# Second feed-forward matmul: the loads of every odd chunk moved from the SyncE and ScalarE queues to the GpSimd queue

## Chip, cores and metric

The kernel runs on all 8 cores of one Trainium2 chip, one batch element per core, with no traffic between the cores. The metric is the device time of the slowest core in microseconds (us). One execution in a comparison is one such time.

## What is computed

One adaLN layer on x of shape 8 x 2048 x 1024 (batch, tokens, width). The part that matters here is the end of it, the feed-forward block with quantized operands:

```python
def bitlinear(x, W, b):
    w_scale = clip(mean(abs(W)), EPS)
    Wq = clip(round(W / w_scale), -1, 1) * w_scale          # ternary weights
    x_scale = clip(max(abs(x), axis=-1), EPS)
    xq = clip(round(x * (127 / x_scale)), -128, 127) * (x_scale / 127)
    return einsum('bnd,hd->bnh', xq, Wq) + b

h = layernorm(x) * (1 + cb) + sb
h = gelu(bitlinear(h, W1, b1))          # 1024 -> 4096
x = x + gb * bitlinear(h, W2, b2)       # 4096 -> 1024, the part around the change
```

Before it stand the modulation vectors (silu(c) @ wmod), a first layernorm and a gated recurrence over the tokens (three 1024 x 1024 projections and a scan).

## The kernel before

Each core works on its element transposed: the width lies on the 128 partitions, the 2048 tokens in the free dimension. `Prog` collects the instructions of each engine as a list written out by hand; `p.on(engine, fn, wait, inc)` appends waits on semaphores and then the instruction. An engine works strictly through its list, so an instruction whose wait isn't met holds up all behind it on that engine. `dma=True` only takes away the serializing wait that ScalarE, VectorE and GpSimd put around their own compute instructions. A DMA adds 16 to its semaphore when it has landed.

The second matmul multiplies the quantized hidden activations (4096 x 2048, bf16, 16 MB, kept in HBM as `h1qsp`) with the ternary weights (4096 x 1024, kept as `w2qsp`). The eight PSUM banks `PB` hold two output blocks of 128 rows (`d0`, `d1`) times four token tiles of 512. So the output is made in four groups `gi` = 0 to 3 of two blocks each, and each group reads all 32 chunks `kc` of the contraction again.

- Group 0 (matmuls at L1292) is made while VectorE quantizes the activations pair by pair; each pair is stored to `h1qsp` (L1279).
- Groups 1 to 3 (matmuls at L1332) only load and multiply. A chunk is 8 matmuls of 128 x 128 by 128 x 512 and needs two loads: its activations `H1Q2[pp]` <- `h1qsp[kc]`, 128 x 2048 bf16, 512 KB, issued by SyncE at L1319 (in the profile: X<-h1qsp, engine SPq), and its weights `W2R[pp]` <- `w2qsp[kc]`, 128 x 1024 bf16, 256 KB, issued by ScalarE at L1321 (M<-w2qsp and RB<-w2qsp, engine ACTq). There are four buffers of each, `pp` = `kc % 4`. The load of chunk kc waits for the matmuls of chunk kc-4; the first four of a group wait for the last matmul of the group before, and in group 1 also for the last stores of `h1qsp`.
- After each group follows an epilogue of eight tiles `ei` over two output buffers `OUTP`: VectorE scales PSUM, ScalarE applies gate and bias, VectorE adds the residual, GpSimd issues the store to `out_img` (L1368). Tile ei waits for the store of tile ei-2, which used the same buffer. The first matmul of the next group waits until VectorE has read the last bank.

So at the end of a group SyncE prefetches four activation chunks at once, while ScalarE comes to the four weight loads only behind its eight epilogue activations, and GpSimd has nothing but the stores.

Of the kernel before, what the change touches and what calls it, by code (L numbers as in the profile page):

```python
# [106 lines left out]
def build_nc():  # L107
    nc = bass.Bass("TRN2", target_bir_lowering=False)
    p = Prog()
# [39 lines left out]
    h1qsp = nc.dram_tensor("h1qsp", [HC, 128, L], BF16, kind="Internal").ap()  # L149
# [80 lines left out]
    for _j, _v in enumerate(_cvals):  # L230
# [8 lines left out]
    PB = [nc.alloc_psum_tensor(f"PB{i}", [128, NT], F32).ap() for i in range(8)]  # L239

    semnames = ["sBR", "sMD", "sM1", "sM2", "sM3", "sLXa", "sLXb", "sCN", "sWMa", "sWMb", "sLWa", "sLWb",
                "sMW", "sW1a", "sW1b", "sW2", "sW2b", "sW2c", "sW2d", "sLWc", "sLWd", "sSP", "sSPa", "sSPb", "sRDa", "sRDb",
                "sFINa", "sFINb", "sMM", "sDV", "sAC", "sPL",
                "sVq", "sSq", "sPq", "sTAP", "sH1a", "sH1b", "sW1c", "sW1d"]
    sems = {s: nc.alloc_semaphore(s) for s in semnames}
# [1 line left out]
    for s in semnames:  # L247
# [7 lines left out]
         inc=("sCN", 16), dma=True)  # L255
    p.on("scalar", lambda E: E.dma_start(out=CPB[:], in_=cpack_b),
         inc=("sCN", 16), dma=True)
    p.on("scalar", lambda E: E.dma_start(out=IDNF[:], in_=idnf),
         inc=("sCN", 16), dma=True)
# [3 lines left out]
    for k in range(KC):  # L263
# [3 lines left out]
             wait=w, inc=(sx, 16))  # L267
        p.on("vector", lambda E, k=k: E.tensor_copy(chunk(X, k), xstg[k % 2]),
             wait=[(sx, p.cnt[sx])], inc=("sDV", 1))
# [3 lines left out]
         wait=[("sCN", cn_all)], inc=("sAC", 1))  # L273
# [143 lines left out]
    for t in range(48):  # L417
# [4 lines left out]
            inc=("sMD", 1) if t == 47 else None)  # L422
    mm_modc = p.cnt["sMD"]
    p.on("vector", lambda E: E.tensor_copy(MODC[:], PB[2][:, 0:48]),
         wait=[("sMD", mm_modc)], inc=("sDV", 1))
# [43 lines left out]
    def ws2_fin(E):  # L469
# [10 lines left out]
         wait=[("sDV", ws2_done)])  # L480
    p.on("tensor", lambda E: E.matmul(PB[7][:, 1:2], ONESRf[:],
                                      WSrow[0:1, 3:4], start=True, stop=True),
         inc=("sMM", 1))
# [11 lines left out]
    for k in range(KC):  # L495
        wv = [("sDV", modc_done)] if k == 0 else []
        for j in range(NNT):
# [3 lines left out]
                wait=wv if j == 0 else [],  # L501
                inc=("sM3", 1) if (k == KC - 1 and j == NNT - 1) else None)
# [17 lines left out]
    for k in range(KC):  # L520
        wv = [("sM3", st1_mm[k - 2])] if k >= 2 else []
        p.on("vector", lambda E, k=k: E.tensor_tensor(
            sq1[k % 2], chunk(X, k), chunk(X, k), ALU.mult),
            wait=wv, inc=("sDV", 1))
        sqdv = p.cnt["sDV"]
        for j in range(NNT):
# [4 lines left out]
                wait=[("sDV", sqdv)] if j == 0 else [],  # L531
                inc=("sM3", 1) if j == NNT - 1 else None)
# [28 lines left out]
    for j in range(NNT):  # L561
# [3 lines left out]
            wait=[("sAC", rstd1_ac)] if j == 0 else [],  # L565
            inc=("sM3", 1) if j == NNT - 1 else None)
# [10 lines left out]
    for j in range(NNT):  # L577
# [3 lines left out]
            wait=[("sAC", bc1e_ac)] if j == 0 else [],  # L581
            inc=("sM3", 1) if j == NNT - 1 else None)
# [12 lines left out]
    for k in range(KC):  # L595
        wv = [("sDV", bc1_done)] if k == 0 else [("sAC", p.cnt["sAC"])]

        def ln_apply_v(E, k=k, src=X):
# [6 lines left out]
            wait=[("sDV", p.cnt["sDV"])], inc=("sAC", 1))  # L605
# [79 lines left out]
    if DEBUG_TAPS:  # L685
        p.on("gpsimd", lambda E: E.dma_start(out=tap_hln, in_=Hh[:]),
             wait=[("sAC", p.cnt["sAC"])], inc=("sTAP", 16), dma=True)
        p.on("gpsimd", lambda E, v=p.cnt["sTAP"]: E.wait_ge(sems["sTAP"], v))
        p.on("gpsimd", lambda E: E.dma_start(out=tap_mod, in_=MODC[:]),
             inc=("sTAP", 16), dma=True)  # L690
# [160 lines left out]
    for k in range(KC):  # L851
        wv = [("sDV", bc2_done)] if k == 0 else []

        def h2_v(E, k=k):
# [6 lines left out]
            wait=[("sDV", p.cnt["sDV"])], inc=("sAC", 1))  # L861
        acn = p.cnt["sAC"]
        M1n = XS(4096, 6144)
        if k == 0:
# [3 lines left out]
                wait=[("sAC", acn)], inc=("sDV", 1))  # L868
        else:
# [3 lines left out]
                wait=[("sAC", acn)], inc=("sDV", 1))  # L873
# [4 lines left out]
        inc=("sDV", 1))  # L878
# [100 lines left out]
    if DEBUG_TAPS:  # L979
        p.on("gpsimd", lambda E: E.dma_start(out=tap_xq, in_=Hh[:]),  # L980
             wait=[("sDV", p.cnt["sDV"])], inc=("sTAP", 16), dma=True)
        def tapstm(E):
# [4 lines left out]
             inc=("sTAP", 16), dma=True)  # L987
        p.on("gpsimd", lambda E, v=p.cnt["sTAP"]: E.wait_ge(sems["sTAP"], v))
        p.on("gpsimd", lambda E: E.dma_start(out=tap_bs[:, L:2 * L], in_=BS1[:]),
             inc=("sTAP", 16), dma=True)  # L990
# [46 lines left out]
    for hc in range(HC):  # L1037
        if hc + 2 < HC:
            emit_tern(hc + 2)
        for j in range(NNT):  # L1040
            jp = (hc * NNT + j) % 4
            gidx = hc * NNT + j
            for k in range(KC):
                wv = []
                if k == 0:
                    wv = [tern_dvs[hc]]
                    if gidx == 0:
                        wv += [("sDV", xq_done)]
                    if gidx >= 4:
# [6 lines left out]
                     wait=wv, inc=("sMM", 1) if k == KC - 1 else None)  # L1056
# [5 lines left out]
                wait=[("sMM", mmn)], inc=("sDV", 1))  # L1062
# [6 lines left out]
                wait=[("sDV", dvn)], inc=("sAC", 1))  # L1069
        gelu_acs.append(p.cnt["sAC"])  # L1070
        H1T = H1Tp[hc % 2]
        if hc == 0:
# [3 lines left out]
                 wait=[("sAC", gelu_acs[-1])], inc=("sDV", 1))  # L1076
# [22 lines left out]
        inc=("sDV", 1))  # L1099
# [95 lines left out]
    for gi, (d0, d1) in enumerate([(0, 1), (2, 3), (4, 5), (6, 7)]):  # L1195
# [111 lines left out]
        else:  # L1307
            for kc in range(HC):
                pp = kc % 4
                srd = ["sRDa", "sRDb", "sW1a", "sW1b"][pp]  # L1310
                wv = []
                if kc < 4:
                    wv = [("sMM", last_mm)]
                    if gi == 1:
                        wv += [("sH1a", p.cnt["sH1a"]),
                               ("sH1b", p.cnt["sH1b"])]
                elif (gi, kc - 4) in mm_vals:
                    wv = [("sMM", mm_vals[(gi, kc - 4)])]
                p.on("sync", lambda E, kc=kc, pp=pp: E.dma_start(  # L1319
                    out=H1Q2[pp], in_=h1qsp[kc]), wait=wv, inc=(srd, 16))  # L1320
                p.on("scalar", lambda E, kc=kc, pp=pp: E.dma_start(  # L1321
                    out=W2R[pp], in_=w2qsp[kc]), wait=wv, inc=(srd, 16),
                    dma=True)
                rdn = p.cnt[srd]
                mmw = [(srd, rdn)]
                if kc == 0:
                    mmw += [("sDV", bank_free_dv)]
                for nt in range(NNT):
                    for di, d in enumerate((d0, d1)):
                        p.on("tensor",  # L1330
                             lambda E, kc=kc, pp=pp, nt=nt, di=di, d=d:
                             E.matmul(PB[4 * di + nt][:, :],  # L1332
                                      W2R[pp][:, d * 128:(d + 1) * 128],
                                      H1Q2[pp][:, nt * 512:(nt + 1) * 512],
                                      start=(kc == 0), stop=(kc == HC - 1)),
                             wait=mmw if (nt == 0 and di == 0) else [],
                             inc=("sMM", 1) if (nt == NNT - 1 and di == 1)
                             else None)
                mm_vals[(gi, kc)] = p.cnt["sMM"]
# [145 lines left out]
```

How the kernel before makes its waits and increments, by code:

```python
    def on(self, eng, fn, wait=(), inc=None, dma=False):  # L40
        sems = self.sems
        serialized = (eng in ("vector", "scalar", "gpsimd")) and not dma
        for (s, v) in wait:
            if v > 0:
                self.ops[eng].append(lambda E, s=s, v=v: E.wait_ge(sems[s], v))
        if inc is not None:
            sname, amt = inc
            val = self.inc(sname, amt)
            if fn is None:
                self.ops[eng].append(
                    lambda E, s=sname, a=amt: E.sem_inc(sems[s], a))
            elif serialized:
                def run(E, f=fn, s=sname, a=amt):
                    f(E)
                    E.ser_flush_wait()
                    E.sem_inc(sems[s], a)
                self.ops[eng].append(run)
            else:
                self.ops[eng].append(
                    lambda E, f=fn, s=sname, a=amt: f(E).then_inc(sems[s], a))
            return val
        assert fn is not None
        self.ops[eng].append(fn)
        return None
# [1 line left out]
    def barrier(self):  # L66
        for e in ENGINES:
            self.inc("sBR", 1)
        target = self.cnt["sBR"]
        sems = self.sems
        for e in ENGINES:
            self.ops[e].append(lambda E: E.sem_inc(sems["sBR"], 1))
            self.ops[e].append(lambda E: E.wait_ge(sems["sBR"], target))
# [16 lines left out]
    def ser_flush_wait(self):  # L90
        if self._n:
            self._e.wait_ge(self._s, self._n)
```

## Time and profile before

| | us |
|---|---|
| time, median of 2 runs | 2635.03 (2634.61 to 2635.45) |
| the profiled execution, its own time | 2630.86 |
| its span, slowest core (core 6) | 2629.2 |
| spans of the 8 cores | 2607.7 to 2629.2 |
| PE busy | 931.2 (35%) |
| DVE busy | 1413.5 (54%) |
| ACT busy | 529.0 (20%) |
| POOL busy | 192.2 (7%) |
| mean granted TensorE clock, core 6 | 0.684 |

PE is TensorE's matmuls, PEld its weight loads, DVE VectorE, ACT ScalarE, POOL GpSimd, SP SyncE; a q behind the name is the engine's sequencer. The DMA queues are called q1 (issued by SyncE), q10 (by ScalarE) and q0 (by GpSimd). Times in rows are us from the span's start, all on core 6. Groups 1 to 3 with their epilogues run from about 2304.9 us to the end, which is 324 of the 2629 us.

### The profile page before, as it was taken

How to read it: one execution, taken by the hardware profiler on the slowest of the kernel's cores; microseconds unless marked ns; L12 is line 12 of the kernel's file. 1: busy time of each engine (PE TensorE's matmuls, PEld its weight loads, DVE VectorE, ACT ScalarE, POOL GpSimd, SP SyncE). 2: the span in 40 equal slices, each digit the busy share in tenths (PEclk: the TensorE clock that was granted, in tenths of full speed). 3: DMA queues.
4: the chain of work that ended last, by engine and by line, in shares of the span. 5: the costliest groups of instructions: out<-in, count | busy, mean ns of one | idle time of the engine just before them, and what ended most of it. 6: DMA issues, size and time to landing. Idle time of an engine off the chain costs nothing.

```text
span 2629.2 us, 14779 instructions; the slowest of 8 cores (2607.7 to 2629.2 us)
## 1 busy us (share of the span) xinstructions
PE 931.2 (35%) x3428; PEld 337.7 (13%) x3428; DVE 1413.5 (54%) x1180; ACT 529.0 (20%) x452; POOL 192.2 (7%) x180
## 2 busy tenths in 40 slices
PE   0772333554543010047777110101101011074754
PEld 0110011221220000013333000000000000021211
DVE  1000033335534658876666665999999999601011
ACT  0202322412333221113232102122121221000000
POOL 0000000101000000023223110000000000000000
PEclk9895566876776555578999655655555555596978
DMA  6765300110000000012222661212112121295965
GB/s 202 269 220 190 145 0 24 48 48 24 24 24 32 0 0 0 0 64 105 105 105 80 221 186 48 80 40 80 56 63 80 40 80 56 76 306 179 312 228 194
DMA packets 71846, 265.45 MB, mean 101 GB/s; under 512 B 7632, under 2 KB 8016, under 8 KB 64336
## 3 DMA queue, kind: packets, MB, share of 16 engines
q1 hardware_dynamic: 36896, 155.20, 17.2%
q0 software_dynamic: 18304, 67.12, 7.0%
q10 hardware_dynamic: 16560, 42.19, 4.9%
q8 instruction: 29, 0.48, 0.1%
q14 instruction: 57, 0.47, 0.1%
HBM read 214.15 MB, written 50.33 MB: 101 GB/s over the span
## 4 chain that ended last, share of the span: by engine, by line
DVE 48%; DMA 18%; PE 13%; ACT 10%; issue 8%; DVEq 2%; POOL 1%; ACTq 1%; SPq 0%; POOLq 0%
DVE X L100 21%; DVE Hh L100 12%; DVE SC L100 7%; PE PB L734 6%; DMA SC<-w2T 4%; DMA RB<-w2qsp 3%; PE PB L1332 3%; ACT X L100 2%; DVE M L100 2%; DMA M<-w2qsp 2%; ACT SC L100 2%; DMA out_img<-SC 2%; DMA SC<-xT 2%; ACT WSB L100 2%; PE PB L306 2%
## 5 line engine op out<-in xcount | busy, mean ns | idle before, releaser
L100 DVE TENSOR_TENSOR SC<-PB,BS 128x512 f32<-128x512 f32 x160 | 110.7, 692 | 316.0 <-PE PB L1332 238.1
L734 PE MATMUL PB<-Hh,WSB 128*128 128x512 bf16 x768 | 190.5, 414 | 189.1 <-POOLq L56 133.1
L100 DVE TENSOR_TENSOR X<-X 128x2048 bf16<-128x2048 bf16 (+1 forms) x120 | 206.8, 1723 | 15.7 <-DVE X L100 2.2
L1052 PE MATMUL PB<-Hh,W1Q 128*128 128x512 bf16 x512 | 123.4, 403 | 227.3 <-POOLq L56 193.7
L1292 PE MATMUL PB<-Hh,M 128*128 128x512 bf16 x128 | 46.3, 541 | 307.0 <-DVEq L56 307.0
L100 DVE TENSOR_SCALAR X<-X 128x2048 bf16<-128x2048 bf16 (+1 forms) x145 | 139.0, 959 | 24.2 <-DVE Hh L100 4.9
L100 ACT ACTIVATE X<-X 128x4096 bf16<-128x4096 bf16 (+1 forms) x24 | 73.2, 3048 | 372.5 <-DVEq L56 371.5
L1292 PE MATMUL PB<-X,RB 128*128 128x512 bf16 x128 | 45.1, 530 | 280.4 <-DVEq L56 280.4
L1332 PE MATMUL PB<-X,M 128*128 128x512 bf16 x384 | 98.6, 406 | 117.1 <-DMA M<-w2qsp 114.9
L100 ACT ACTIVATE X<-SC,CPF 128x512 bf16<-128x512 f32 x128 | 92.4, 722 | 216.6 <-DVEq L56 214.4
L1052 PE MATMUL PB<-Hh,RB 128*128 128x512 bf16 x512 | 120.9, 397 | 33.7 <-DVEq L56 33.7
L100 DVE TENSOR_TENSOR Hh<-Hh 128x4096 bf16<-128x4096 bf16 x56 | 128.4, 2292 | 5.8
L734 PEld LDWEIGHTS PB<-Hh,WSB 128*128 128x128 bf16 x768 | 79.6, 105 | 300.5 <-issue 225.7
L100 ACT ACTIVATE Hh<-Hh 128x4096 bf16<-128x4096 bf16 x16 | 57.9, 3617 | 247.5 <-DVEq L56 246.8
L100 ACT ACTIVATE SC<-SC,B2G,GBt 128x512 f32<-128x512 f32 x32 | 26.0, 813 | 385.6 <-DVEq L56 385.6
L100 DVE TENSOR_SCALAR Hh<-Hh 128x4096 bf16<-128x4096 bf16 x72 | 88.4, 1227 | 18.3 <-ACTq L56 7.8
L1332 PE MATMUL PB<-X,RB 128*128 128x512 bf16 x384 | 89.9, 378 | 22.7 <-DMA RB<-w2qsp 21.6
L100 DVE SCALAR_TENSOR_TENSOR X<-X 128x4096 bf16<-128x4096 bf16 (+1 forms) x24 | 89.1, 3714 | 2.5
L1052 PEld LDWEIGHTS PB<-Hh,W1Q 128*128 128x128 bf16 x512 | 51.5, 102 | 299.0 <-issue 248.3
L306 PE MATMUL PB<-WSTG,SCf 128*1 128x512 f32 x96 | 49.5, 675 | 65.3 <-DMA WSTG<-wmodT 64.0
L100 DVE SCALAR_TENSOR_TENSOR Hh<-Hh 128x4096 bf16<-128x4096 bf16 x16 | 70.8, 4425 | 1.7
L100 POOL TENSOR_TENSOR W1Q<-SC 128x1024 bf16<-128x1024 f32 x16 | 37.5, 2344 | 461.1 <-DVEq L56 449.1
(172 smaller groups left out, 1396.5 us busy)
## 6 DMA issues: line engine op xcount, KB each, us to landing
X<-h1qsp SPq DMA_DIRECT2D x96, 512.0 KB, 6.2
SC<-w1T POOLq DMA_DIRECT2D x32, 512.0 KB, 6.1
WSTG<-w1T SPq DMA_DIRECT2D x32, 512.0 KB, 3.3
h1sp<-X POOLq DMA_DIRECT2D x32, 512.0 KB, 3.0
WSTG<-wmodT SPq DMA_DIRECT2D x6, 2048.0 KB, 11.3
SC<-wmodT SPq DMA_DIRECT2D x12, 1024.0 KB, 9.2
SC<-w2T SPq DMA_DIRECT2D x12, 1024.0 KB, 8.0
M<-w2qsp ACTq DMA_DIRECT2D x48, 256.0 KB, 6.7
```

Source lines behind the costliest of these rows:

```text
L100: ins = f(*a, **k)
L306: p.on("tensor", lambda E, j=j, k=k: E.matmul(PB[j % 2][0:1, :], SCf[:, k:k + 1], mod_piece(j, k), start=(k == 0), stop=(k == KC - 1)), wa ...
L734: E.matmul(PB[pp + gi][:, :], WSB[:, gi * 1024 + k * 128: gi * 1024 + (k + 1) * 128], ntile(Hh, k, j), start=(k == 0), stop=(k == KC - 1)),
L1052: E.matmul(PB[jp][:, :], w1q[hc % 4][:, k * 128:(k + 1) * 128], ntile(Hh, k, j), start=(k == 0), stop=(k == KC - 1)),
L1292: E.matmul(PB[4 * di + nt][:, :], W2R[2 * pf + kch][:, d * 128:(d + 1) * 128], FIN[pf][:, kch * 2048 + nt * 512: kch * 2048 + (nt + 1) * 512],
L1332: E.matmul(PB[4 * di + nt][:, :], W2R[pp][:, d * 128:(d + 1) * 128], H1Q2[pp][:, nt * 512:(nt + 1) * 512], start=(kc == 0), stop=(kc == HC ...
```

## The change

In groups 1 to 3 the loads of even chunks stay where they are (activations on SyncE, weights on ScalarE). Both loads of every odd chunk are issued by GpSimd, activations first, then weights, with the same waits on the matmuls. Odd chunks get two semaphores of their own in place of sRDb and sW1b. Sizes, buffers and the count of loads stay the same.

```diff
@@ -1307,7 +1307,7 @@
-                srd = ["sRDa", "sRDb", "sW1a", "sW1b"][pp]
+                srd = ["sRDa", "sGRa", "sW1a", "sGRb"][pp]
@@ -1316,9 +1316,12 @@
-                p.on("sync", lambda E, kc=kc, pp=pp: E.dma_start(
-                    out=H1Q2[pp], in_=h1qsp[kc]), wait=wv, inc=(srd, 16))
-                p.on("scalar", lambda E, kc=kc, pp=pp: E.dma_start(
+                heng = "sync" if kc % 2 == 0 else "gpsimd"
+                weng = "scalar" if kc % 2 == 0 else "gpsimd"
+                p.on(heng, lambda E, kc=kc, pp=pp: E.dma_start(
+                    out=H1Q2[pp], in_=h1qsp[kc]), wait=wv, inc=(srd, 16),
+                    dma=True)
+                p.on(weng, lambda E, kc=kc, pp=pp: E.dma_start(
                     out=W2R[pp], in_=w2qsp[kc]), wait=wv, inc=(srd, 16),
                     dma=True)
```

The lines of the changed kernel are three higher: its activations are loaded at L1321, its weights at L1324, its matmuls are L1335 and its stores L1371.

GpSimd at the border of groups 0 and 1, before (-) and now (+). L1279 is the store of the quantized activations, L1368 and L1371 the stores of the output; sMM counts matmul chunks, sDV VectorE's steps, sH1a and sH1b the stores to `h1qsp`.

```order
 L1279 DMA h1qsp<-Hh 128x2x2048 [waits sDV]
 L1279 DMA h1qsp<-X 128x2x2048 [waits sDV]
-L1368 DMA out_img<-SC 128x512 [waits sDV] x32
-L1378 UNCONDITIONAL_BRANCH
+L1371 DMA out_img<-SC 128x512 [waits sDV] x8
+L1321 DMA X<-h1qsp 128x2048 [waits sMM,sH1a,sH1b]
+L1324 DMA M<-w2qsp 128x1024 [waits sMM,sH1a,sH1b]
+L1321 DMA X<-h1qsp 128x2048 [waits sMM,sH1a,sH1b]
+L1324 DMA RB<-w2qsp 128x1024 [waits sMM,sH1a,sH1b]
+L1321 DMA X<-h1qsp 128x2048 [waits sMM]
```

The loads of chunks 1 and 3 now stand behind the eight stores of the epilogue, and then 14 more odd chunks follow before the next eight stores. The same holds at the borders of groups 1 and 2 and of groups 2 and 3.

ScalarE at a border of groups, before: behind the eight activations of the epilogue come the weights of chunks 0 and 1 (buffer M1, called M), 2 and 3 (RB), and so on.

```order
L100 ACTIVATE SC<-SC,B2G,GBt 128x512 x8
L1321 DMA M<-w2qsp 128x1024 x2
L1321 DMA RB<-w2qsp 128x1024 x2
L1321 DMA M<-w2qsp 128x1024 x2
L1321 DMA RB<-w2qsp 128x1024 x2
```

The same place now:

```order
L100 ACTIVATE SC<-SC,B2G,GBt 128x512 x8
L1324 DMA M<-w2qsp 128x1024
L1324 DMA RB<-w2qsp 128x1024
L1324 DMA M<-w2qsp 128x1024
L1324 DMA RB<-w2qsp 128x1024
```

Of each pair of weight loads one is left. On SyncE, 48 activation loads stand in a row where there were 96.

## Rows read from the trace of the kernel before

**Rows 1.** The page, part 2: busy tenths of the DMA engines in 40 slices

```profile
DMA  6765300110000000012222661212112121295965
```

**Rows 2.** Busy time by stretch, core 6: an epilogue, then group 2

```profile
core 6: us, PE busy (x) PEld busy (x) DVE busy (x) ACT busy (x) POOL busy (x), PEclk, DMA share, GB/s
2382.70:2416.60 33.90, 0.00 (x0) 0.00 (x1) 11.08 (x16) 6.50 (x8) 4.32 (x8) 0.54 0.40 133
2416.60:2491.00 74.40, 60.84 (x256) 23.32 (x256) 0.00 (x0) 0.00 (x0) 0.00 (x0) 0.98 0.92 307
```

**Rows 3.** Waits from 2304 to 2600 us: total us, times, longest us

```profile
PE PB L1332 <- DMA M<-w2qsp: 114.9, 24, 34.1
PE PB L1332 <- DMA RB<-w2qsp: 21.6, 30, 1.6
DVE SC L100 <- DMA out_img<-SC: 15.2, 10, 3.8
```

**Rows 4.** Chain that ended last, four chunks inside group 2: start, us, what

```profile
2433.61 1.90 PE PB L1332 x8
2435.58 7.20 DMA RB<-w2qsp
2442.92 1.90 PE PB L1332 x8
```

**Rows 5.** DMA, 2425 to 2480 us: packets, MB, share of 16 engines by queue

```profile
DMA packets 6753, 18.53 MB, mean 337 GB/s; under 512 B 740, under 2 KB 740, under 8 KB 6751
...
q1 hardware_dynamic: 3392, 12.38, 65.1%
q10 hardware_dynamic: 3359, 6.12, 34.5%
```

**Rows 6.** Timeline, border of groups 1 and 2: start, us, engine line op

```profile
2382.64 41.08 SPq L1319 DMA_DIRECT2D X<-h1qsp  x7
2382.81 0.69 DVE L100 TENSOR_TENSOR SC<-PB,BS 128x512 f32<-128x512 f32 x1 [82.17 <-PE PB L1332]
2383.76 0.81 ACT L100 ACTIVATE SC<-SC,B2G,GBt 128x512 f32<-128x512 f32 x1 [84.07 <-DVEq L56]
...
2386.18 0.54 POOL L1368 DMA_DIRECT2D out_img<-SC  x1 [84.34 <-DVEq L56]
...
2392.37 0.69 DVE L100 TENSOR_TENSOR SC<-PB,BS 128x512 f32<-128x512 f32 x1 [3.81 <-DMA out_img<-SC]
...
2411.85 0.81 ACTq L1321 DMA_DIRECT2D M<-w2qsp  x2
2411.91 0.69 DVE L100 TENSOR_TENSOR SC<-SC,X 128x512 f32<-128x512 f32 x1 [1.33 <-ACTq L56]
...
2413.26 0.54 POOL L1368 DMA_DIRECT2D out_img<-SC  x1 [2.51 <-DVEq L56]
...
2416.63 4.96 PE L1332 MATMUL PB<-X,M 128*128 128x512 bf16 x16 [34.07 <-DMA M<-w2qsp]
```

**Rows 7.** DMA by queue, from 2388 to 2389 us

```profile
q1 hardware_dynamic: 91, 0.33, 89.3%
```

**Rows 8.** DMA by queue, from 2390 to 2391 us

```profile
q0 software_dynamic: 93, 0.33, 80.6%
q1 hardware_dynamic: 36, 0.10, 24.5%
```

**Rows 9.** Timeline, last epilogue: the third tile's first VectorE step

```profile
2605.05 0.69 DVE L100 TENSOR_TENSOR SC<-PB,BS 128x512 f32<-128x512 f32 x1 [0.34 <-DMA out_img<-SC]
```

**Rows 10.** DMA issues of L1319 (SyncE): ns min/median/max, count, landing

```profile
L1319 SPq DMA_DIRECT2D X<-h1qsp x96: 319/320/385, 2271.4 to 2589.1; - x96
...
DMA to landing us min/median/max: 3.3/6.2/8.3
```

**Rows 11.** DMA issues of L343 (GpSimd, 512 KB loads of w1T early on), likewise

```profile
L343 POOL DMA_DIRECT2D SC<-w1T x32: 528/528/683, 1.6 to 306.3; - x32
...
DMA to landing us min/median/max: 3.5/6.1/14.6
```

**Rows 12.** DMA by queue, 196 to 310 us: GpSimd's loads of w1T

```profile
q0 software_dynamic: 3024, 11.01, 27.3%
```

More of the change, by code:

```diff
@@ L241, in build_nc @@
     semnames = ["sBR", "sMD", "sM1", "sM2", "sM3", "sLXa", "sLXb", "sCN", "sWMa", "sWMb", "sLWa", "sLWb",
-                "sMW", "sW1a", "sW1b", "sW2", "sW2b", "sW2c", "sW2d", "sLWc", "sLWd", "sSP", "sSPa", "sSPb", "sRDa", "sRDb",
+                "sMW", "sW1a", "sW1b", "sGRa", "sGRb", "sW2", "sW2b", "sW2c", "sW2d", "sLWc", "sLWd", "sSP", "sSPa", "sSPb", "sRDa", "sRDb",
                 "sFINa", "sFINb", "sMM", "sDV", "sAC", "sPL",
```

## Prediction

> **What bounds the kernel now.** I read the page's slices first, because the change touches only the last eighth of the span. The DMA engines stand at 9 tenths in three stretches near the end [rows 1]: groups 1 to 3 of the second matmul. Between them the digits fall to 5 or 6, where a slice is half epilogue. The table by stretch then separates the two kinds [rows 2]. Group 2 takes 74.4 us, in which PE is busy 60.84 us at a clock of 0.98 and the DMA engines are busy for 92% of the time. The epilogue ahead of it takes 33.9 us, with PE at nothing and DVE busy for 11.08 us.
>
> The waits say what ends last [rows 3]: PE waits for loads 136.5 us in all. Three long waits, one per epilogue, with 34.1 us the longest, are about 100 us of it; the other 51 are short, some 0.7 us each, one for every second chunk or so. The chain inside a group shows a regular lap [rows 4]: a chunk's 8 matmuls (1.90 us), then the load that takes their buffer (7.20 us to its landing), then the next matmuls from that buffer. A lap is 2442.92 - 2433.61 = 9.31 us for four chunks, 2.33 us per chunk. Is this bound by the load's latency or by bandwidth? The queues answer [rows 5]: 65.1% + 34.5% = 99.6% of all 16 engines' time is used, at 337 GB/s. A chunk is 512 KB + 256 KB = 0.786 MB, and 0.786 MB / 337 GB/s = 2.33 us. So the groups are bound by bandwidth, and the 7.20 us are mostly waiting behind other chunks. Who issues a load does not enter that number.
>
> The epilogue is a chain through VectorE, ScalarE, VectorE and the store. In it one wait is odd [rows 6]: the first store is issued at 2386.18, and VectorE's third tile, which needs its buffer, starts only at 2392.37 after 3.81 us idle. In the last epilogue, with no prefetch beside it, the same step waits 0.34 us [rows 9].
>
> **The change, step by step.**
>
> 1. *Two activation chunks leave the prefetch.* SyncE issues four chunks (2.10 MB) from 2382.64 on. From 2388 to 2389 q1 holds 89.3% of the engines and q0 does not appear although its store was issued two microseconds before [rows 6, 7]; it moves its data from about 2390 [rows 8]. The store is served behind the reads that came first. With chunks 0 and 2 alone, 1.05 MB less stands ahead of it. At 337 GB/s that is 3.1 us; the most there is to win is 3.81 - 0.34 = 3.47 us. I take 3.0 us, three times (ahead of groups 1, 2 and 3): **-9.0 us**, with bounds 0 and -10.4.
>
> 2. *The odd loads of a group's start come late.* Chunks 1 and 3 now stand behind GpSimd's last store (2413.26 + 0.54 = 2413.8), 31 us later than their activations were issued before. Their four loads are 1.57 MB, or 4.7 us of DMA. In their favour: 0.52 MB of weights that ScalarE issued at 2411.85 are among these and no longer in its queue, so what is new to this stretch is 1.05 MB, 3.1 us. Is there room? PE starts at 2416.63, and its first 16 matmuls take 4.96 us where two chunks inside the group take 3.8 [rows 4, 6]. No load of chunk 4 can be issued before chunk 0 is done, some 3 us after the start. In that hole the DMA engines have only weights to fetch. So chunk 1 lands at about 2413.8 + 1.5 (two issues and the start of the data) + 0.786/337 + 0.5 (completion) = 2418 to 2419, when PE is still in chunk 0, and chunk 3 some 2.3 us later, ahead of its turn. What is left is a queue that is a little longer when chunk 4 joins. I take 0.5 us per group, **+1.5 us**; bounds 0, and 3 x 3.1 = +9.3 if none of it is hidden.
>
> 3. *The odd loads inside a group.* 16 pairs per group, 48 in all. On GpSimd an issue takes 0.53 us against SyncE's 0.32 [rows 10, 11]. GpSimd reacts later: VectorE's step ends at 2412.60 and GpSimd's issue starts at 2413.26, 0.66 us; ScalarE started 0.26 us after the end of VectorE's first step (2383.50 to 2383.76) [rows 6]. An undisturbed 512 KB load lands in 3.5 us at best against 3.3. And the weights wait for the issue of the activations. Together 0.40 + 0.53 + 0.2 + 0.2 = 1.3 us later than before. GpSimd itself has time: 2 x 0.53 us in a pair's 4.66 us. What hides the 1.3 us is the backlog at the DMA engines. Of a lap's 9.31 us, about 0.4 (reaction and issue) + 1.7 (3.3 us less 512 KB at 337 GB/s) + 1.9 (matmuls) = 4.0 us are not service, so 5.3 us of the lap go to the DMA engines' queue, where a chunk's own service needs 2.3. The cover is 3.0 us, and 1.3 is less. I take **0**; bounds 0 and one full 1.3 us per lap, 24 laps, +31 us.
>
> 4. *Cost per byte.* In the groups q1 and q10 need 0.996 x 55 x 16 / 18.5 = 47.4 us of one engine per MB [rows 5]. q0's loads needed 0.273 x 114 x 16 / 11.01 = 45.2 [rows 12]. Half of 25.2 MB per group by 2.2 / 16 is 1.7 us per group, -5.2 us for three. But the rows of q0 come from a stretch where the engines rested more than half the time, so the gap may be contention and not the queue. I take **0**; bounds 0 and -5.2.
>
> 5. *The rest.* VectorE and ScalarE do nothing inside the groups [rows 2], so nothing waits behind the moved loads. GpSimd's eight stores at a group's end stand behind the last odd load, which was issued four chunks before. The last epilogue has no loads behind it and stays.
>
> The sum: -9.0 + 1.5 = -7.5 us. The profiled execution took 2630.86 us (span 2629.2), so it would take 2623.4; its median in the runs is 4.2 us above, which gives **2627.5 us**. A change below 2% (53 us) is about what a measurement of this kernel can't tell from none, and all of this lies below.
>
> The Trainium skill (DMA: Bandwidth & Descriptors, "Issuing engines are not separate DMA queues") says that DMAs from all issuing engines end up on the same 16 DMA engines, so spreading them over more issuers saves issue time alone. The trace agrees that issue time is not the limit: 0.32 us for a load against 2.33 us for a chunk. By this rule step 4's gain would be nothing, which is what the sum has.
>
> The page also says ("Queues, rings and completion order") that each engine serves its rings in turn, packet by packet. The trace differs at the first store: q0 got nothing while q1's older reads were under way [rows 7]. By the rule the first store would already share the engines today, and an odd chunk on one ring would be served more slowly than an even chunk on two; this is the last rival below.
>
> **The rivals.**
>
> - *The third queue moves bytes faster.* A gain in step 4. For it: 45.2 against 47.4. Against it: the engines are at 99.6% already, and q0's number is from a quieter stretch. It gives 2627.5 - 5.2 = 2622.
> - *The lost prefetch is paid and nothing is won.* The first store's delay would be the neighbour core's traffic or the first store's own, and the 1.05 MB per group are paid in full: 2635.0 + 3 x 3.1 = 2644. For it: VectorE's ten waits for stores in [rows 3] come to 15.2 us, and the two waits of 3.8 us that lie in that stretch explain only half; the other eight come with no prefetch beside them. Against it: rows 7 and 8 show whose bytes go first, and rows 9 show the same step without them.
> - *The odd landing paces the lap.* Slower than before. If the DMA queues run dry once per lap, the 1.3 us of step 3 are paid 24 times: 2627.5 + 31 = 2659. It decides from the point where an odd load comes later than the 3.0 us that the backlog covers. Even and odd loads being on different queues makes the backlog uneven: with two even chunks landed, q0 may hold the only work. For it: an average says nothing of the lowest point. Against it: 1.3 is under half of 3.0, and if an even chunk is served first PE has work in hand at once when the odd one lands.
> - *The rings share by turns.* An odd chunk on q0 then gets 4 KB in 10 while an even one is queued on q1 and q10, and can end as much as a chunk's service later, 2.33 us. With 1.3 that is 3.6 us, above the cover. Paid in full in 24 laps it is 87 us: 2715. Against it: rows 7 and 8.
>
> **How the numbers follow.** The forecast has 0.54, the faster queue 0.12, the lost prefetch 0.10, the pacing by odd landings 0.20, the sharing 0.04. The forecast's own range is 2617 to 2640, from the bounds of steps 1 and 2. The range goes to 2614 at the low end (the faster queue with step 1 at its bound) and to 2662 at the high end (the odd landings paid in full). Over 2% faster would need 53 us; the three groups' gap between DMA time and PE time is only 3 x (74.4 - 60.8) = 41 us, so 0.01. Over 2% slower is the last rival alone, 0.04. Within 2%: 0.95.
>
> **What would show it.** Right: VectorE's third tile in the three first epilogues waits under 1 us in place of 3.8; the epilogues shrink by about 3 us; a group still takes 74 to 76 us with DMA at 9 tenths and over 330 GB/s; q0 carries half the bytes. The landing times of L1321 and L1324 on GpSimd may well be longer without harm. Wrong: groups of 80 us or more, GB/s under 320 inside them, digits of 8 and below, PE waiting mostly for loads of odd chunks with waits over 2 us followed by an even chunk at once. If the long wait of 3.8 us stays, step 1 is wrong. If chunk 1 of a group comes over 2 us late, step 2 is.

## The result, and the profile after

| | before | after |
|---|---|---|
| time, median | 2630.70 us (10 runs) | 2649.17 us (11 runs) |
| ratio, 95% interval | | 1.0057 (1.0039 to 1.0076) |
| the profiled execution, its own time | 2630.86 | 2638.35 |
| its span, slowest core | 2629.2 (core 6) | 2636.7 (core 1) |
| POOL busy | 192.2 | 243.1 |

The change makes the kernel slower by 0.57%, about 15 us by the ratio and 18 us by the medians. The forecast was 3 us faster than the 2630.7 here (7.5 us faster by its own sum). The time lies inside the range of the prediction, on the other side of before.

The slices of the page, DMA engines, after, which answer to [rows 1]:

```profile
DMA  6765401010000000022231851211212111396774
```

Where three stretches of 9 tenths stood there is one 9, and then 6 7 7 4. The table by stretch, core 1, shows the epilogue and group 2, against [rows 2]:

```profile
core 1: us, PE busy (x) PEld busy (x) DVE busy (x) ACT busy (x) POOL busy (x), PEclk, DMA share, GB/s
2379.70:2409.40 29.70, 0.05 (x1) 0.03 (x1) 11.07 (x16) 6.52 (x8) 6.45 (x12) 0.59 0.35 120
2409.40:2490.40 81.00, 62.53 (x256) 24.96 (x256) 0.00 (x0) 0.00 (x0) 14.89 (x28) 0.94 0.90 293
```

The pause of PE shrank from 33.9 to 29.7 us, and the group grew from 74.4 to 81.0. PE itself is busy hardly longer (62.5 against 60.8 us), and the bytes per second fell from 307 to 293. The waits from 2290 to 2640 us, core 1, beside [rows 3] (total us, times, longest us):

```profile
POOL X L1321 <- PE PB L1335: 179.2, 42, 9.3
PE PB L1335 <- DMA M<-w2qsp: 114.7, 22, 29.9
...
PE PB L1335 <- DMA RB<-w2qsp: 29.1, 23, 2.5
DVE SC L100 <- DMA out_img<-SC: 11.3, 15, 1.6
```

The longest short wait of PE is now 2.5 us, where it was 1.6. VectorE's longest wait for a store is 1.6 us, where it was 3.8.

From the trace of all eight cores I take two numbers per kernel: the length of a group (first matmul to the end of the last) and the idle time of PE between groups. Before, they are 75.55 and 32.49 us on average, after 82.73 and 28.73. Three groups at +7.2 us and three pauses at -3.8 us make +10 us on an average core. The time counts the slowest of eight cores, and it rose by 15. The profiled execution after is one of the quick ones, 2638.35 us where the median is 2649.17.

**The start of a group.** The timeline of core 1 at the border of groups 0 and 1, after, beside [rows 6]:

```profile
2293.22 0.34 ACTq L1324 DMA_DIRECT2D M<-w2qsp  x1
...
2294.53 0.54 POOL L1371 DMA_DIRECT2D out_img<-SC  x1 [3.29 <-DVEq L56]
2295.16 0.54 POOL L1321 DMA_DIRECT2D X<-h1qsp  x1
2295.78 0.54 POOL L1324 DMA_DIRECT2D M<-w2qsp  x1
2296.38 0.54 POOL L1321 DMA_DIRECT2D X<-h1qsp  x1
2296.99 0.54 POOL L1324 DMA_DIRECT2D RB<-w2qsp  x1
2297.22 3.57 PE L1335 MATMUL PB<-X,M 128*128 128x512 bf16 x8 [29.88 <-DMA M<-w2qsp]
...
2302.75 3.57 PE L1335 MATMUL PB<-X,M 128*128 128x512 bf16 x8 [1.96 <-DMA M<-w2qsp]
```

Chunk 1 is loaded from 2295.16 on, behind the last store, and lands 7.5 us later. PE is through with chunk 0 at 2300.79, waits 1.96 us and then runs chunk 1 at the lower clock as well (3.57 us for 8 matmuls at a granted clock of 0.50, which is the 1.2 GHz level, where 1.89 us are usual inside a group). Over all 24 starts of a group chunk 1 lands 5.7 to 8.2 us after GpSimd's issue, 6.6 us in the mean.

**The middle of a group.** The DMA queues of core 1 from 2425 to 2480 us, after, for [rows 5] (packets, MB, share of 16 engines):

```profile
DMA packets 5832, 17.94 MB, mean 326 GB/s; under 512 B 733, under 2 KB 733, under 8 KB 5829
...
q0 software_dynamic: 2576, 9.09, 52.5%
q1 hardware_dynamic: 1616, 5.85, 29.3%
q10 hardware_dynamic: 1637, 2.97, 16.8%
```

That is one of the better stretches. In a bad one the engines have nothing to do. The timeline of core 1, inside group 1:

```profile
2335.72 1.89 PE L1335 MATMUL PB<-X,M 128*128 128x512 bf16 x8 [1.96 <-DMA M<-w2qsp]
2337.44 3.62 PE L1335 MATMUL PB<-X,RB 128*128 128x512 bf16 x16
2338.14 0.53 POOL L1321 DMA_DIRECT2D X<-h1qsp  x1 [6.49 <-PE PB L1335]
2338.67 0.54 POOL L1324 DMA_DIRECT2D M<-w2qsp  x1
2339.41 3.77 SPq L1321 DMA_DIRECT2D X<-h1qsp  x2
2339.41 0.35 ACTq L1324 DMA_DIRECT2D RB<-w2qsp  x1
2340.89 1.89 PE L1335 MATMUL PB<-X,M 128*128 128x512 bf16 x8
```

And the DMA engines of the same core from 2339 to 2341 us, in 40 slices:

```profile
DMA  2123101101000000000000000000000900999990
...
DMA packets 28, 0.06 MB, mean 28 GB/s; under 512 B 10, under 2 KB 10, under 8 KB 28
```

From 2339.55 to 2340.55 us no packet is under way. PE waited for an odd chunk until 2335.72. By then the chunks behind it had landed or were about to, so it runs on without a pause, and all four pairs of buffers are full or in use. The next odd load can be issued only when the odd chunk is done, GpSimd starts that issue at 2338.14, 0.53 us after the matmuls' end at 2337.61 (SyncE and ScalarE start theirs at 2339.41, 0.1 us after the next chunk ends), and the first packet of it starts at 2340.55, 2.4 us after the issue.

Over the middle of the groups (chunks 9 to 27), summed over the packets in the trace of each core, the DMA engines are busy for 1.00 of the time before and 0.94 after. Their time per MB rose only from 48.1 to 48.6 us. Stretches in which no packet at all is under way make 0.7 us of this part of a group after and 0.0 before; the rest of the missing 6% are moments in which some of the 16 engines rest.

### The profile page after: what moved, and what is told of

Read it like the earlier page. It is cut to its first block, busy times and chain, and to the rows that moved or that the text cites. A ratio compares the mean times of both kernels' runs of the same rounds, so it can differ in the third digit from the quotient of the medians.

```text
span 2636.7 us, 14779 instructions; the slowest of 8 cores (2624.7 to 2636.7 us)
## 1 busy us (share of the span) xinstructions
PE 933.9 (35%) x3428; PEld 341.5 (13%) x3428; DVE 1412.1 (54%) x1180; ACT 529.6 (20%) x452; POOL 243.1 (9%) x276
## 4 chain that ended last, share of the span: by engine, by line
DVE 48%; DMA 17%; PE 13%; ACT 10%; issue 8%; DVEq 2%; POOL 1%; ACTq 1%; SPq 0%; POOLq 0%
DVE X L100 21%; DVE Hh L100 12%; DVE SC L100 7%; PE PB L734 6%; DMA SC<-w2T 4%; DMA M<-w2qsp 4%; PE PB L1335 3%; ACT X L100 2%; DVE M L100 2%; DMA RB<-w2qsp 2%; ACT SC L100 2%; DMA SC<-xT 2%; ACT WSB L100 2%; PE PB L306 2%; ACT Hh L100 2%
## 5 line engine op out<-in xcount | busy, mean ns | idle before, releaser
L1292 PE MATMUL PB<-Hh,M 128*128 128x512 bf16 x128 | 46.8, 546 | 307.1 <-DVEq L56 307.1
L1292 PE MATMUL PB<-X,RB 128*128 128x512 bf16 x128 | 45.6, 535 | 279.9 <-DVEq L56 279.9
L1335 PE MATMUL PB<-X,M 128*128 128x512 bf16 x384 | 100.7, 413 | 115.0 <-DMA M<-w2qsp 114.7
L1335 PE MATMUL PB<-X,RB 128*128 128x512 bf16 x384 | 96.3, 400 | 29.3 <-DMA RB<-w2qsp 29.1
L891 PE MATMUL PB<-IDNF,SC 128*128 128x128 f32 x32 | 8.2, 425 | 180.4 <-DVEq L56 180.4
```

The source lines that it names most:

```text
L891: p.on("tensor", lambda E, blk=blk, b4=b4, tgt=tgt: E.transpose(tgt[:, b4 * 128:(b4 + 1) * 128], SC[0][:, blk * 128:(blk + 1) * 128], IDNF ...
L1292: E.matmul(PB[4 * di + nt][:, :], W2R[2 * pf + kch][:, d * 128:(d + 1) * 128], FIN[pf][:, kch * 2048 + nt * 512: kch * 2048 + (nt + 1) * 512],
L1335: E.matmul(PB[4 * di + nt][:, :], W2R[pp][:, d * 128:(d + 1) * 128], H1Q2[pp][:, nt * 512:(nt + 1) * 512], start=(kc == 0), stop=(kc == HC ...
```

## The experiments

The table has all runs. Group and pause are means over eight cores of the profiled execution, as above; the pause is taken at the two borders between groups 1, 2 and 3. The three stages of a group are means over the cores with complete matmul records. The DMA share is the sum of the packets' times, which can overlap a little. The ratio is to the kernel before on the same chip, with its 95% interval.

| | ratio | group | pause | chunks 0-4 | 4-8 | 8-28 | DMA |
|---|---|---|---|---|---|---|---|
| before | | 75.6 | 32.5 | 9.3 | 9.7 | 47.3 | 1.00 |
| after | 1.0057 (1.0039, 1.0076) | 82.7 | 28.7 | 11.8 | 10.6 | 50.3 | 0.94 |
| e1_start_only | 1.0008 (0.998, 1.0036) | 78.8 | 29.8 | 12.0 | 10.3 | 47.4 | 1.00 |
| e2_body_only | 1.0061 (1.0033, 1.0089) | 80.5 | 33.0 | 9.1 | 11.3 | 51.3 | 0.91 |
| e3_two_rings | 1.0012 (0.9978, 1.0046) | 76.6 | 33.2 | 9.0 | 10.7 | 48.0 | 0.97 |
| e4_acts_only | 1.0026 (0.9995, 1.0058) | 76.5 | 32.9 | 9.1 | 10.3 | 48.3 | 0.99 |
| e5_late_rings | 1.0109 (1.0051, 1.0166) | 83.5 | 32.1 | 9.5 | 10.9 | 53.5 | 0.88 |
| e6_ring8_before | 1.0001 (0.9971, 1.003) | 73.7 | 33.4 | 9.4 | 9.7 | 46.8 | 1.01 |
| e7_ring8_after | 1.0007 (0.9977, 1.0037) | 76.2 | 30.9 | 12.0 | 11.6 | 45.2 | 1.00 |
| e8_out4 | 0.9927 (0.9904, 0.9949) | 76.4 | 27.4 | 9.5 | 10.1 | 47.6 | 1.00 |
| e9_late_start | 0.9973 (0.9953, 0.9993) | 77.9 | 29.5 | 10.7 | 10.7 | 48.0 | 1.00 |
| e10_out4_early | 0.9882 (0.9844, 0.9921) | 76.6 | 22.5 | 9.9 | 9.9 | 47.9 | 1.00 |
| e11_best | 0.9813 (0.9769, 0.9857) | 70.4 | 23.2 | 9.0 | 6.9 | 45.5 | 1.00 |

Theory A came from the traces above: a late start and a slower middle cost time, a shorter epilogue gives some back.

### Only the start, only the middle

e1_start_only leaves GpSimd only chunks 1 and 3 of a group; e2_body_only leaves it the odd chunks from 5 on. What GpSimd doesn't load goes back to SyncE and ScalarE, with the semaphores of before.

```diff
 e1_start_only
-                heng = "sync" if kc % 2 == 0 else "gpsimd"
-                weng = "scalar" if kc % 2 == 0 else "gpsimd"
+                heng = "gpsimd" if kc in (1, 3) else "sync"
+                weng = "gpsimd" if kc in (1, 3) else "scalar"
 e2_body_only
+                heng = "gpsimd" if kc % 2 and kc > 3 else "sync"
+                weng = "gpsimd" if kc % 2 and kc > 3 else "scalar"
```

> Only chunks 1 and 3 of each group are loaded by GpSimd, chunks 5 to 31 as before. Theory A (the loss has two places, a late start of each group of about 3.5 us and a slower body of about 3.2 us, and the shorter epilogue gives 3.8 us back): the epilogues between groups are about 28.8 us of PE idle time, the groups about 79 us, and the time is that of before within 3 us. Rival B (the body alone loses, and the start only looks late because the queue behind it is): groups 75.5 us and a time some 11 us below before.

> Chunks 1 and 3 of each group are loaded as before, the odd chunks from 5 on by GpSimd. Theory A: PE idles 32.5 us between groups again (VectorE's third tile waits 3.8 us), the groups take about 78.7 us, and the time is 10 to 15 us above before. Rival B (the whole loss of 6.7 us per group is in the body): groups 82 us, 20 us or more above before. Rival C (the body's loss comes only from the late start, as a lag that is carried on): groups 75.5 us, the time of before.

With the start alone Theory A's numbers came: the groups are 78.8 us, the pauses 29.8, and the time is that of before (median 2639.74 against 2634.96, ratio 1.0008). With the middle alone the pauses are back at 33.0 us and the whole loss stands, 1.0061, which is 16 us (20 by the medians). Its groups are 80.5 us, between the 78.7 of Theory A and the 82 of rival B: without the late start the middle loses 4.0 us in chunks 8 to 28 and 1.7 in chunks 4 to 8. So the lag of the start isn't what slows the middle, and rival C falls by e2. Rival B falls by e1, where the start alone makes the groups 3.2 us longer and the expected gain of 11 us isn't there. Start and epilogue cancel.

### Is it GpSimd, or one queue for one chunk?

e3_two_rings uses no GpSimd load. From chunk 4 on, SyncE issues both loads of an odd chunk and ScalarE both of an even one.

```diff
-                heng = "sync" if kc % 2 == 0 else "gpsimd"
-                weng = "scalar" if kc % 2 == 0 else "gpsimd"
+                heng = "sync" if kc % 2 or kc < 4 else "scalar"
+                weng = "sync" if kc % 2 and kc > 3 else "scalar"
```

> From chunk 4 on, both loads of an odd chunk are issued by SyncE and both of an even chunk by ScalarE; nothing on GpSimd, chunks 0 to 3 as before. It has the changed kernel's split of a chunk (one queue for one chunk, weights issued behind activations) without GpSimd. Theory A with a cause in GpSimd (it issues 0.7 us after the matmuls end where SyncE takes 0.1, and needs 0.53 us per issue): groups 75.5 us and the time of before within 3 us. Rival D (one chunk on one queue is what loses, since the chunks finish out of turn): groups 78 us or more, 8 us or more above before.

The groups are 76.6 us, 1.0 above before, and the time is not told apart from before. So the way in which a chunk is put on one queue costs something (the engines are down at 0.97 of the middle), but only a fifth of what e2 loses. Rival D's 8 us are out.

e4_acts_only moves the activations of the odd chunks from 5 on alone.

```diff
+                heng = "gpsimd" if kc % 2 and kc > 3 else "sync"
+                weng = "scalar"
```

> From chunk 5 on, only the activations of odd chunks are issued by GpSimd, their weights by ScalarE; chunks 0 to 3 as before. Theory A with lateness as the cause: the second issue behind the first (0.53 us) is gone, 0.7 us of late reaction stay, so about half of the body's 3.2 us per group: groups 77 us, 4 to 7 us above before. Rival E (bytes on the software queue cost more time at the DMA engines, or land more unevenly): two thirds of the body's loss, in proportion to the bytes, groups 77.6 us, 6 to 10 us above before. The two lie close; the busy share of the DMA engines tells them apart, below 0.96 by lateness, 0.98 or more by cost per byte.

The groups came out at 76.5 us, below what either side expected, with DMA at 0.99 and 48.5 us per MB. The time, 1.0026 (about 7 us), fits both sides and isn't clear of none. By the sign set beforehand the DMA share of 0.99 speaks for rival E, a cost per byte, but in this run the bytes on q0 cost less engine time than the others (45.4 us per MB). So with GpSimd's late reaction on the activations alone 0.9 us per group is lost; with the weights behind them on the same queue, e2, it is 4.9, more than this and e3's 1.0 together: the cost isn't proportional to the delay. That neither number was met says that I still had no right size for the cover.

### Lateness without GpSimd

e5_late_rings is e3 with later odd loads: they wait for half of the next chunk's matmuls, about a microsecond.

```diff
                     wv = [("sMM", mm_vals[(gi, kc - 4)])]
+                    if kc % 2:
+                        wv = [("sMH", mh_vals[(gi, kc - 3)])]
...
                              inc=("sMM", 1) if (nt == NNT - 1 and di == 1)
+                             else ("sMH", 1) if (nt == 1 and di == 1)
                              else None)
```

> As e3_two_rings (no load on GpSimd), but an odd chunk's two loads wait for the first 4 of the 8 matmuls of the chunk after the one whose buffers they take, so SyncE issues them at least 0.95 us later. Theory L (lateness of the odd loads alone empties the DMA engines' queue): groups of 79 to 81 us against 76.6 in e3 and 80.5 in e2, the DMA engines busy for about 0.92 of the body, 8 to 15 us above before. Rival Q (something of GpSimd's queue itself, as its cost per byte or its uneven landing): groups 76.6 to 77.5 us, DMA busy 0.96 or more, within 5 us of before.

The loss is there without a byte on q0, and it is larger: groups of 83.5 us, ratio 1.0109. Theory L expected 79 to 81, so the delay was stronger than GpSimd's: both loads of an odd chunk are at least 0.95 us late here, where in the changed kernel the activations are issued 0.46 us later than in the kernel before and the weights 0.98 us (the delay of e5 also grows whenever PE waits ahead of the chunk waited for). The queues of core 6 from 2435 to 2490 us, in e5:

```profile
DMA  9979966996999899924799999999927999998229
...
DMA packets 5764, 15.77 MB, mean 287 GB/s; under 512 B 641, under 2 KB 641, under 8 KB 5762
...
q1 hardware_dynamic: 2883, 7.89, 44.9%
q10 hardware_dynamic: 2879, 7.86, 42.2%
```

44.9% + 42.2% = 87%. The digits 2 4, 2 and 2 2 among the nines are holes of the same kind as in the changed kernel.

### More chunks in flight

e6 and e7 give the ring eight buffers, in the kernel before and in the changed one.

```diff
-    H1Q2 = [XS(0, 2048), XS(2048, 4096), XS(4096, 6144), XS(6144, 8192)]
+    H1Q2 = [XS(i * 2048, (i + 1) * 2048) for i in range(8)]
+    (W2R: also MB and W1Q in halves)
-                pp = kc % 4
+                pp = kc % 8
...
-                elif (gi, kc - 4) in mm_vals:
-                    wv = [("sMM", mm_vals[(gi, kc - 4)])]
+                elif kc < 8:
+                    wv = [("sMM", mm_vals[(gi, 0)])]
+                else:
+                    wv = [("sMM", mm_vals[(gi, kc - 8)])]
```

> The kernel before with eight buffers in place of four for activations and weights; chunks 0 to 3 are loaded as before, 4 to 7 once chunk 0 is done, from 8 on each waits for the chunk eight earlier. The DMA engines are at 1.00 in the body already, so both theories expect the groups at 75.5 us, at most 1 us less from an earlier chunk 4 to 7, and the time of before within 3 us. It is the base for the next run.

> The changed kernel with the same eight buffers. Theory L (lateness, covered by too short a queue of outstanding loads): with twice the chunks in flight the DMA engines are busy for 0.99 or more of the body, chunks 8 to 28 take 47.5 us as in before (50.3 in the changed kernel), and only the late start of some 2.5 us per group is left: groups about 78 us, PE idle 28.8 us between them, the time of before within 4 us. Rival Q (cost per byte or uneven landing of GpSimd's queue): the body stays at 49.5 us or more, groups 81 us, 6 to 10 us above before.

Before gains nothing that can be measured. The changed kernel gets its middle back: chunks 8 to 28 take 45.2 us, from 50.3, and the time is that of before (1.0007). The queues of core 2 in e7, from 2430 to 2485 us:

```profile
DMA  9999999999999999999999999999999999999996
...
q0 software_dynamic: 2921, 10.23, 51.6%
q1 hardware_dynamic: 1705, 6.19, 31.0%
q10 hardware_dynamic: 1729, 3.13, 16.6%
```

99.2% in all, with more than half of the bytes on q0. GpSimd is exactly as late as in the changed kernel (0.54 us after the matmuls' end in both); with eight chunks in flight that costs nothing in the middle. There a MB costs 46.7 us of engine time here and 47.6 in e6, so q0's bytes aren't dearer. The cores of e7 are of two sorts, and why is open: cores 1, 2 and 5 take 43 to 43.5 us for chunks 8 to 28 and pause for 32 to 34 us, the other five take 45.8 to 48.5 us and pause for 28 to 31; core 2, shown above, is of the first sort. All eight are below the 50.3 us of the changed kernel. Of rival Q the cost per byte is out. Its other half, the uneven landing, isn't told apart from the late issue by this run: both make an odd chunk land late, and eight buffers would hide both. e5 shows only that a late issue alone is enough for a loss of this size. The late start is left: 12.0 us for the first four chunks.

### The wait for the store, by itself

e8_out4 takes the kernel before, and doubles the output buffers instead of cutting the prefetch.

```diff
-    OUTP = [SC[2][:, 0:512], SC[2][:, 512:1024]]
+    OUTP = [SC[2][:, i * 512:(i + 1) * 512] for i in range(4)]
...
-            pp = ei % 2
+            pp = ei % 4
...
-            if ei >= 2 or gi >= 1:
+            if ei >= 4 or gi >= 1:
```

> The kernel before with four output buffers in the epilogue in place of two, so that a tile waits for the store of four tiles earlier; all loads as before. It takes the wait of 3.8 us behind the prefetch away and leaves the prefetch whole. Theory A: groups 75.5 us, PE idle between them 27.5 to 28.5 us where it was 32.5 (eight tiles at about 3.05 us and the first weights), the last epilogue 1 us shorter, together 12 to 16 us below before. Rival F (the third tile's wait hides another one of the same length, for ScalarE or PSUM): under 5 us below before.

Ratio 0.9927, 19 us, a little more than expected: the pauses fall to 27.4 us and the groups are 76.4, 0.8 us above before. VectorE's third tile waits 0.3 us where it waited 4.0 (means over 24 epilogues). That is the gain of the change's first step without its price.

### The late start, by itself

e9_late_start leaves everything on SyncE and ScalarE, but the activations of chunks 1 and 3 wait for VectorE's last step of the epilogue.

```diff
+                for hk in {0: [0, 2], 2: []}.get(kc, [kc]):
+                    hp = hk % 4
+                    hv = wv + [("sDV", prev_evac_dv)] if hk in (1, 3) else wv
-                p.on("sync", lambda E, kc=kc, pp=pp: E.dma_start(
-                    out=H1Q2[pp], in_=h1qsp[kc]), wait=wv, inc=(srd, 16))
+                    p.on("sync", lambda E, hk=hk, hp=hp: E.dma_start(
+                        out=H1Q2[hp], in_=h1qsp[hk]), wait=hv,
+                        inc=(["sRDa", "sRDb", "sW1a", "sW1b"][hp], 16))
```

> The kernel before, all loads on SyncE and ScalarE, but the activations of chunks 1 and 3 wait for the last VectorE step of the epilogue, as they do in effect in the changed kernel; chunks 0 and 2 are loaded as before. Theory A (the late issue makes both the gain in the epilogue and the loss at the group's start, GpSimd's queue has no part in either): PE idles 29 to 30 us between groups, the first four chunks of a group take 11 to 12 us where they took 9.3, the groups about 78 us, the time of before within 4 us. Rival S (the loss at the start is GpSimd's landing): the first four chunks take 10 us or less and the time is 5 us or more below before.

The pause is 29.5 us, so the gain in the epilogue has nothing to do with GpSimd. But the first four chunks take 10.7 us where e1 has 12.0 and before has 9.3, and the kernel is 0.27%, 7 us, faster than before. So the time missed Theory A's 4 us and met the 5 us of rival S, while the 10.7 us lie between the two: the late issue makes about half of the loss at the start. The other half goes with GpSimd. Its first issue starts 1.2 us after VectorE's last step, behind the last store, where SyncE in e9 starts 0.2 us after it; and its four issues follow one another in 2.4 us, each chunk's weights behind its activations, while in e9 ScalarE had issued the weights ahead. Which of these counts most wasn't tried.

### Faster than both

e10_out4_early is e8 with the weights of chunks 0 to 3 issued by SyncE beside the activations. e11_best adds the eight buffers and loads chunks 4 to 7 during the epilogue as well, each behind one step of VectorE.

```diff
 e10_out4_early
-                p.on("scalar", lambda E, kc=kc, pp=pp: E.dma_start(
+                p.on("sync" if kc < 4 else "scalar", lambda E, kc=kc, pp=pp: E.dma_start(
 e11_best
+                p.on("sync" if kc < 8 else "scalar", lambda E, kc=kc, pp=pp: E.dma_start(
...
+                elif kc < 8:
+                    wv = [("sDV", add_vals[kc - 1])]
```

> As e8_out4, and SyncE also issues the weights of chunks 0 to 3, right behind each activation load, so they no longer wait for ScalarE's last activation. PE then waits for the last bank alone: PE idle between groups of 22 to 24 us where e8 had 27.4, groups of 75.5 us, and a time of 28 to 34 us below before. If the 1.05 MB more ahead of the first stores come back as a wait (rival), the idle time stays above 26 us and the time less than 22 us below before.

> As e10, with eight buffers, and SyncE loads chunks 4 to 7 during the epilogue too, each behind one VectorE step of it. 6.3 MB of a group's 25.2 MB then move while the DMA engines would rest, and 18.9 MB at 337 GB/s are 56 us, less than PE's 61 us: the groups become bound by PE, 63 to 67 us, PE idle between them 23 to 26 us, 50 to 65 us below before. Rival: the loads slow the stores so much that the epilogue gives back over half of it, under 30 us below before.

e10 has a median of 2605.51 us beside 2633.02 of before, ratio 0.9882, which is 31 us by the ratio and as expected, with groups of 76.6 us. e11 has 2588.30 us, ratio 0.9813, 45 us below by the medians and 49 by the ratio, where 50 to 65 were expected. In e11 the DMA engines work through the pause. Its epilogue and group 2, core 4:

```profile
2365.70:2388.60 22.90, 0.06 (x2) 0.07 (x2) 10.39 (x15) 5.72 (x8) 3.78 (x7) 0.56 0.91 251
2388.60:2459.70 71.10, 60.14 (x251) 23.75 (x256) 0.69 (x1) 0.78 (x1) 0.54 (x1) 0.97 0.94 303
```

0.91 of the pause where [rows 2] had 0.40. The groups come to 70.4 us, not to the 63 to 67 expected. They are still bound by the DMA engines, which were slower per MB here (49.6 us in the middle, 322 GB/s). Why they are slower wasn't tried; all cores now load at the same time for longer, which is an argument and not a measurement.

## Why the prediction was wrong, step by step

**Step 1, the shorter prefetch: right.** The prediction took -3.0 us, bounded at 3.47 by the wait alone. Over the 24 epilogues ahead of groups 1 to 3 the third tile's wait fell from 4.0 us (3.0 to 5.7) to 0.8 us (0.5 to 1.6), in the mean under the 1 us that was named as the sign. The longest of them is on core 1, in the first epilogue:

```profile
2274.80 0.69 DVE L100 TENSOR_TENSOR SC<-PB,BS 128x512 f32<-128x512 f32 x1 [1.59 <-DMA out_img<-SC]
```

The pause fell by 3.8 us. Of that 3.4 us lie between VectorE's first and last read of PSUM (27.3 to 23.9 us), and 0.3 us between the last read and the first matmul. e9 and e8 confirm the mechanism from two sides.

**Step 2, the late start: mis-sized.** It had +0.5 us per group. The first four chunks took +2.5, within the bound of 3.1. The working let chunk 1 land 4 to 5 us after GpSimd's first issue, before chunk 0 ends; it took 6.6 us in the mean. The working gave chunk 1 the engines for its own 0.786 MB. When it had landed, q0 had moved 1.4 to 1.8 MB since that issue, at most 0.26 of them for the last store, so at least 0.3 MB of chunk 3 had gone with it. PE waits 1.8 us for chunk 1 in the mean of the 18 starts with complete records (over 2 us at 6 of them), and not at all before. Nor did the sum count that a stall there keeps PE at the lower clock into a second chunk: its 8 matmuls take 2.9 us in the mean, 2.4 before.

**Step 3, the odd loads inside a group: this step failed.** It had 0, hidden by a cover of 3.0 us. The mechanism was named as the third rival, at 1.3 us a lap, and the runs support it: e5 makes the loss without GpSimd, and e7 takes it away with GpSimd. The lateness was read nearly right: GpSimd starts an issue 0.54 us after the matmuls' end and SyncE 0.08, a difference of 0.46 where 0.40 was taken, and the weights follow 0.5 us behind. It was the cover that was wrong. Chunks 4 to 28 took +4.0 us per group, 0.7 us for each of these six laps, half of the rival's full price of 1.3. The sum and the rival both used an average. A lap's 5.3 us in the queue are only there on average if the chunks finish evenly. Here they finish in bunches: a late odd chunk holds PE while the chunks behind it land, PE then eats them without a pause, and at that moment nothing is outstanding. The cover to count is the least work outstanding, not the mean. How much of the late landing comes from the late issue and how much from the uneven landing told of below stays open.

**Step 4, cost per byte: right to take 0.** In the middle q0's bytes cost 50.3 us per MB after and 46.6 in e7, so a rate read from one state of the engines says little about another. With all queues together it rose by 0.5 us per MB after.

The sum with the measured terms is 3 x (-3.8 + 2.5 + 4.0 + 0.2) = +9 us on the cores with complete records (the 0.2 is that of the last four chunks), +10 over all eight. The measured +15 us is that of the slowest core of each run. What adds the difference wasn't isolated. The slowest core doesn't stand out more than it did: it is 11 us above the mean of its eight cores in the 12 executions after and 13 us above it in the 31 of before that were run beside e1, and between these two sets the mean core is 10.5 us slower (2632.7 against 2622.2). Those 31 have a median of 2634.96 us, where the 10 of the table above have 2630.70; so part of the 15 us may lie in the executions of before that were compared, which isn't shown.

The range doesn't follow from the bounds either. Steps 1 and 2 bound the time at 2635 - 10.4 = 2625 and 2635 + 9.3 = 2644, not at 2617 and 2640; the faster queue takes the low end to 2619, not 2614, and the third rival gives 2659, not 2662. The measured 2649 lies inside by any of these only because the third rival was counted in.

The second rival (nothing won in the epilogue) is out by the 0.8 us of step 1 and by e9, the first (a faster queue) by the engine time per MB, which didn't fall in the changed kernel (48.6 us, 48.1 before). The last one, sharing by turns, isn't needed: e3 puts one chunk on one queue as well, and loses 1.0 us per group.

The rule of the Trainium skill that was weighed (DMA: Bandwidth & Descriptors, "Issuing engines are not separate DMA queues"), that another issuer saves issue time alone, agrees with e7, where half of the chunks on q0 leave the time as it is (ratio 1.0007, beside 1.0001 of e6). It does not speak of an issuer that reacts later, and that is what this change was about.

## What to carry to other kernels

With a ring of few buffers and DMA engines at 100%, the issuer's reaction time counts, although no single issue is near the bound: look for the smallest number of outstanding loads, and add a buffer before adding a queue. A prefetch and a store that someone waits for should not be issued together; more output buffers took that wait away for 0.8 us per group (e8, 19 us faster), where a shorter prefetch gave part of the gain back at the start of the next group (e9, 7 us faster). Work that DMA engines can do in a pause (here weights issued behind ScalarE's last activation) was worth more than a balance between queues: e10 and e11 gained 31 and 49 us.

## What the runs showed of the hardware

- GpSimd starts a DMA issue 0.54 us after the end of the matmuls that it waits for (median in the changed kernel), SyncE and ScalarE 0.08 us. A load's first packet started 2.4 us after GpSimd's issue in the hole shown above, a store's 1.1 us after it in the last epilogue.
- The chunks loaded by GpSimd land less evenly. From the 24th to the last of a chunk's 32 semaphore steps pass 1.3 us in the mean in the changed kernel, against 0.8 for the chunks of the other two queues in the same trace, and 0.8 for all before. In e7 it is 1.9 against 0.9, and the middle is fast all the same: with enough in flight this too costs nothing.
- A store issued behind 2.1 MB of reads on another queue got no share of the engines until those were nearly done [rows 7, 8]: the first store of an epilogue has its first packet 3.2 to 4.4 us after its issue before, at all 24 borders. With half the reads it is 1.1 to 1.5 us, and the third tile's wait fell from 4.0 to 0.8 us.
